# A mixture-of-experts, Mamba and soft-routing kernel: the routing chain's place among the first products on VectorE and TensorE, and five TensorE products on zeros ahead of the first inputs

## The reference, cut to what matters

```python
shared_out = jnp.einsum('nh,dh->nd', jax.nn.silu(x_flat @ sw1.T) * (x_flat @ sw3.T), sw2)
t_bias = t_emb @ router_t_w.T
s = jax.nn.sigmoid((x_flat @ router_w.T + t_bias_flat).astype(jnp.float32))
sel_scores = s + router_bias
_, topk_idx = jax.lax.top_k(sel_scores, TOP_K)
s_sel = jnp.take_along_axis(s, topk_idx, axis=1)
denom = jnp.sum(s_sel, axis=1, keepdims=True)
gates = jnp.where(denom > EPS, s_sel / (denom + EPS), 1.0 / TOP_K)
combine = jnp.sum(gates[:, :, None] * jax.nn.one_hot(topk_idx, N_EXPERTS), axis=1)
H = jax.nn.gelu(jnp.einsum('nd,ehd->enh', x_flat, rw1), approximate=False)
O = jnp.einsum('enh,edh->end', H, rw2)
routed_out = jnp.einsum('end,ne->nd', O, combine)
out = (shared_out + routed_out) / (N_SHARED + TOP_K)
```

## Time and profile before

| what | before |
|---|---|
| median of 3 runs | 1472.04 us (1471.96, 1472.04, 1476.65) |
| the profiled execution | 1476.72 us |
| its span | 1474.9 us |
| PE busy | 1184.5 us, 80% |
| DVE busy | 1149.8 us, 78% |
| ACT busy | 771.7 us, 52% |
| POOL busy | 884.9 us, 60% |
| first stage | about 0 to 187 us |
| the Mamba stage, by the busy shares | about 187 to 1160 us |
| what the change touches | 3.6 to 50 us |

### The profile page before, as it was taken

How to read it: one execution, slowest core, us unless ns; L and a number is a source line. 1 busy time by engine, 2 the same in 40 slices (tenths; PEclk the granted TensorE clock), 3 DMA queues, 4 the chain that set the end, 5 groups by cost and what they waited for, 6 DMA issues and landing times. The chain is left out here.

```text
span 1474.9 us, 14736 instructions
## 1 busy us (share of the span) xinstructions
PE 1184.5 (80%) x4924; PEld 659.2 (45%) x4924; DVE 1149.8 (78%) x1051; ACT 771.7 (52%) x1029; POOL 884.9 (60%) x394
## 2 busy tenths in 40 slices
PE   5999986797639897549986475484598999999998
PEld 3788832232103232113332121131146788787887
DVE  4344459999999999999999999999878654545445
ACT  4444466667645776555775555465256533343330
POOL 4530027999999999999999999999910000000000
PEclk9999998899959898769898678687799999999999
DMA  5344235442463234255123437313015030303012
GB/s 200 107 155 136 95 97 201 157 159 75 162 235 134 99 139 155 101 205 199 72 86 146 154 118 291 142 58 114 13 47 200 24 120 1 143 0 128 0 38 76
DMA packets 46016, 176.34 MB, mean 120 GB/s; under 512 B 5873, under 2 KB 10481, under 8 KB 33538
## 3 DMA queue, kind: packets, MB, share of 16 engines
q1 hardware_dynamic: 45954, 175.57, 32.8%
HBM read 142.78 MB, written 32.77 MB: 119 GB/s over the span
## 5 line engine op out<-in xcount | busy, mean ns | idle before, releaser
L1268 POOL TENSOR_TENSOR scan_dbu<-scan_rep,scan_bc 128x1024 f32<-128x1024 f32 x254 | 592.7, 2361 | 39.6 <-ACT scan_rep L1166 28.7
L1355 DVE TENSOR_TENSOR_SCAN scan_hs<-scan_hs,scan_dbu 128x1024 f32<-128x1024 f32 x191 | 436.7, 2286 | 11.6 <-ACT scan_hs L1193 10.1
L1193 ACT ACTIVATE scan_hs<-scan_rep,scan_neg_a 128x1024 f32<-128x1024 f32 x252 | 280.8, 1118 | 306.1 <-DVE scan_hc L1369 278.7
L1077 PE MATMUL scan_ysum<-scan_hc,scan_sel 128*32 128x512 f32 x1008 | 171.3, 812 | 206.5 <-DVE scan_hc L1369 190.3
L1369 DVE TENSOR_TENSOR scan_hc<-scan_hs,scan_bc 128x1024 f32<-128x1024 f32 x191 | 233.7, 1223 | 6.1
L1077 PEld LDWEIGHTS scan_ysum<-scan_hc,scan_sel 128*32 128x32 f32 x1008 | 35.5, 131 | 320.1 <-issue 269.5
L1274 POOL TENSOR_TENSOR scan_hc<-scan_hc,scan_bc 128x1024 f32<-128x1024 f32 x65 | 153.1, 2356 | 7.6 <-DVE scan_hc L1355 7.4
L1355 DVE TENSOR_TENSOR_SCAN scan_hc<-scan_hs,scan_dbu 128x1024 f32<-128x1024 f32 x65 | 148.1, 2279 | 0.8 <-POOL scan_dbu L1268 0.7
L938 PE MATMUL scan_banks<-late_xin,scan_inwf 128*128 128x512 f32 x256 | 115.2, 604 | 0.0
L32 PE MATMUL ffn_sl<-ffn_tanh_s,xm_s 128*128 128x512 f32 x384 | 107.3, 415 | 2.3 <-DVE ffn_tanh_s L2153 2.3
L1955 PE MATMUL ffn_oy<-ffn_y,ffn_et 128*128 128x256 f32 x448 | 102.0, 379 | 0.8 <-DVE ffn_y L2173 0.8
(11 more groups left out here) (274 smaller groups left out, 1820.4 us busy)
## 6 DMA issues: line engine op xcount, KB each, us to landing
scan_rep<-dd_rows SPq DMA_DIRECT2D x60, 1024.0 KB, 5.7
scan_bc<-bc_rows SPq DMA_DIRECT2D x32, 512.0 KB, 6.0
ffn_wt<-in_ew SPq DMA_DIRECT2D x16, 1024.0 KB, 7.8
dd_rows<-scan_dd SPq DMA_DIRECT2D x15, 1024.0 KB, 3.8
scan_bc<-gate_rows SPq DMA_DIRECT2D x24, 256.0 KB, 4.8
scan_inwf<-fold SPq DMA_DIRECT2D x12, 512.0 KB, 3.8
cond<-scan_bc SPq DMA_DIRECT2D x16, 256.0 KB, 3.1
y_all<-scan_yo SPq DMA_DIRECT2D x6, 512.0 KB, 3.1
```

Of the source, the lines that this page charges most:

```text
L1077: mm = nc.tensor.matmul(ysum[i * D32:(i + 1) * D32, h, :], sel[:], hc[:, (s0 + i) % HCR, h * CT:(h + 1) * CT], start=False, stop=last, til ...
L1193: nc.scalar.activation(hs[:, s % HSR, :], rep[:, e % REPS, 0, :], ACT.Exp, scale=scale).then_inc(da_done, 1)
L1268: nc.gpsimd.tensor_tensor(dbu[:, s % DBR, :], rep[:, e % REPS, 1, :], bc[:, j, 0, :], ALU.mult).then_inc(dbu_done, 1)
L1355: nc.vector.tensor_tensor_scan(states, hs[:, s % HSR, :], dbu[:, s % DBR, :], 0.0, ALU.mult, ALU.add).then_inc(scan_done, 1)
```

## The change

Three things are edited, all in the first stage.

- TensorE runs five products of 128x128 by 128x512 in plain float32 on the zeroed tile comb_wide, after the small products for t_emb and ahead of `value(0)`. It waits for padded first. They write to the bank by_expert, which `logits()` overwrites later; nothing reads what they give.
- VectorE does `low_hidden(0)` ahead of the 14 comparisons, `low_hidden(1)` and `product(2)` right after the rank, `low_hidden(2)` and `product(3)` where `low_hidden(1)` and `product(2)` were, and `low_hidden(3)` before the wait for the turned gates.
- TensorE runs `turn_gates()` two steps later: after `project(2)`, `value(5)` and `project(3)`; `factor(4)` follows `value(6)`.

```diff
@@ TensorE, the start
             mm.then_inc(t_done, 1)
+            pe.wait_ge(padded, 1)
+            for _ in range(IDLE_PRODUCTS):
+                zeros = comb_wide[:].rearrange("p t e -> p (t e)")
+                nc.tensor.matmul(by_expert, zeros[:, 0:P], zeros, start=True, stop=True)
+
@@ TensorE, the order of the first units
             value(4)
-            turn_gates()
             project(2)
             value(5)
+            project(3)
+            turn_gates()
+            value(6)
             factor(4)
-            project(3)
-            value(6)
             factor(5)
@@ VectorE, the routing chain
             link(nc.vector.tensor_tensor(score[:], prob[:], bias[:].unsqueeze(1).to_broadcast([P, NT, EXPERTS]), ALU.add))
-
+            low_hidden(0)
             for e in range(EXPERTS):
...
-            low_hidden(0)
             product(1)
             dve.wait_ge(padded, 1 + EXPERTS)
             dve.wait_ge(chain, links[0])
             link(nc.vector.tensor_reduce(rank[:], beats, AX_X, ALU.add))
+            low_hidden(1)
+            product(2)
             link(nc.vector.tensor_scalar(mask[:], rank[:], float(TOP_K), None, ALU.is_lt))
...
-            low_hidden(1)
-            product(2)
+            low_hidden(2)
+            product(3)
             link(nc.vector.tensor_scalar(den[:], den[:], 1e-9, None, ALU.add))
...
             nc.vector.tensor_tensor(comb, comb, mask[:], ALU.add).then_inc(comb_ready, 1)
-            low_hidden(2)
-            product(3)
+            low_hidden(3)
             dve.wait_ge(gates_turned, 1)
...
-            low_hidden(3)
```

More of the change, by code:

```diff
@@ L59, in moe_phase @@
         HB = 4
+        IDLE_PRODUCTS = 5
         flat = ahead.bc[:].rearrange("p j i t -> p (j i t)")
```

## The result

The kernels were timed side by side, 20 executions each: before 1476.96 us in the median (1471.96 to 1480.91), changed 1472.76 us (1468.33 to 1474.52). The profiled execution spans 4.5 us less, with 22 instructions more. The forecast of 1470.4 us was a gain of 1.6 us on a baseline 4.9 us lower than the one measured beside the change; in us gained it was too small by 2.6.

What follows compares the result with a forecast made beforehand. The first stage was taken as bound by TensorE once routing is over, with waits and half clock ahead of that. Start 1.6 plus middle 0.1 gave 1.7, stated as 1.6: 1472.04 - 1.6 = 1470.4 us, range 1465.8 to 1475.6.

Steps and rivals of the forecast that it cites:

- The start: Ahead of the logits: products on zeros raise TensorE's clock, so value(0) and factor(0) run faster and logits start 1.6 us earlier.
- C: Rival, first stage: the clock raised by the products falls again just ahead of the logits; slower, 1475.6 us; chance 0.14.
- D: Rival, at value(0): the products do nothing, the clock is half at 12.06 and rises where it did; 1472 us; chance 0.08.
- The meeting at 26.17: Last comparison and GpSimd's first rw1 split fall due together; forecast has the comparison first, otherwise the rank ends 2.3 us later.
- The last split: GpSimd's second half of rw2 begins at 33.84 instead of 41.75, stands on L489 or L490, and holds VectorE until 36.3.
- B: Rival, routing: L489 and L490 slip through before the last split, which must come 0.3 us later; 1465.8 us; chance 0.08.
- The wait at `project(2)`: TensorE waits from 32.0 to 37.4, 5.3 us, for low_hidden(2) and falls to 1.2 GHz.
- The sum: Whole kernel: 1.6 from the start plus 0.1 from the middle, 1.7, stated as 1.6 us less.
- The middle: From the logits to project(4): the reordering gives 0.1 us, with 0.8 either way for the clock.
- A: Rival, routing: GpSimd's split comes first at 26.17, the comparison waits, project(1) waits 2.0 us; 1468.6 us; chance 0.28.

Runs made afterwards that it cites:

- the products alone: The kernel before with only the five products on zeros added, both engines' orders as before; 1474.99 us, ratio 0.9997 to before.
- The experiment with 0.2 us more: The changed kernel with one more small VectorE step, its result overwritten, ahead of the 14 comparisons; 1474.44 us, a single execution.
- The run with the split earlier: The changed kernel with ScalarE's high part for the second half of rw2 ahead of hidden(4); 1475.6 us, ratio 0.9998 to before.
- the better order: The changed kernel with low_hidden(2) and product(3) ahead of the mask, rw2's last high half behind hidden(5), turn ahead of project(3); 1469.96 us, ratio 0.9955 to before.
- the run with the later split: The changed kernel with ScalarE's high part for the second half of rw2 behind high_hidden(3); 1472.39 us, ratio 0.9988 to before.
- the order alone: The changed kernel without the five products on zeros; 1475.25 us, ratio 1.0004 to before.
- the run with the turn as before: The changed kernel with TensorE's order as in the kernel before, turn_gates directly behind value(4); 1476.03 us, ratio 1.0008 to before.

## Why the prediction was right and wrong

**The start: right.** 1.6 us forecast, 1.43 measured at the logits. The products end at 10.89, inside the 8.3 to 12.7; `value(0)` takes 1.63, the logits start at 15.79 for 15.6: `factor(0)`, from 14.20, needed 1.59 us for a forecast 1.4. Rivals C and D fall for five products, as the clock held over the waits of 1.16 and 0.52; with two products C's mechanism is there. The size hangs on when the clock rises without such work. The three runs without five products have their logits at 17.22, 17.44 and 16.32, the seven with them at 15.75 to 15.96, so the products give 0.4 to 1.7 us. The gain reached the end of the stage, by the products alone 2.1 us at the next stage's first product.

**The meeting at 26.17: right as forecast, though the prediction said that its rows can't part the two cases.** The comparison came first, the rank is at 25.52 where the 26.95 - 1.43 of the prediction put it, and `project(1)` at 27.80 has no wait. The experiment with 0.2 us more shows how thin that was: it gives the other case. It also bears on what the Trainium skill says ("SBUF — State Buffer", section "Who interferes with whom"), that whoever issues first keeps the shared ports for its whole length; the traces agree, 2.00 us for the comparisons on one side of the meeting, 4.25 on the other. The prediction's own rule, that a routing step stands when all its operands lie in SBUF, is too wide: the rank L489 doesn't (1.21 us beside a split, 1.22 before).

**The last split: this step failed.** The prediction put it at 33.84 in before's count, 32.2 in the changed kernel's, and concluded of L489 and L490 that "both can't be through before it". It began at 32.98. Its start came out of `value(4)` by a chain: `hidden(4)`, ScalarE's half, then the split; and I had `value(4)` follow `project(1)` at once. It does not: `value(4)` needs rw1, whose splits end at 24.75 + 4.87 = 29.62, and it starts at 29.67 though `project(1)` was done by 29.3. The code says so (a wait on `split_done` in `value`), and the earlier trace rows held the time, 30.93 in before's count. I had used that row for VectorE and not for TensorE. The wait is marked as 0.35 us and moves `value(4)` by 0.51: it starts at 29.67 and not at 27.80 + 1.36 = 29.16, where 1.36 is the time of six matmuls from start to start. Of the 0.74 us by which the split came later than forecast it is the largest part; the rest is `project(1)` at 27.80 for 27.7 and `hidden(4)`, 1.69 us behind `value(4)`'s start for a forecast 1.56. Without those 0.51 the split would have begun at 32.47, level with L496. B's condition was that the split comes late ("0.3 us later than I have it"), and B's mechanism is what came, half: L489 and L490 (now L496 and L497) slipped through, 0.17 us each, but the step behind the next low part, L500, then stood for it, 1.31 us. So `project(4)` is at 45.19, between B's 43.4 and the forecast's 47.9.

**The wait at `project(2)`: wrong by the same step.** 5.3 us forecast at half clock, 2.30 measured at full clock. The run with the split earlier has the forecast's mechanism and its half clock, and there the wait is 3.98: `project(2)` starts at 35.52 for a forecast 37.4 - 1.6 = 35.8, but `value(4)` ends at 31.54, not at 32.0 - 1.6 = 30.4. It is the overlooked wait again. The prediction had said what would refute it: "I'm wrong if the wait at `project(2)` is under 3 us with a short last comparison". That is what came, so its account of the middle is wrong, though the time lies in the range.

**The sum.** The middle was put at 0.1 and gave 2.94. With the start 4.4 us instead of 1.7. The range held the time (1472.76 in 1465.8 to 1475.6), but that the forecast of 1470.4 came within 2.4 of it is partly luck: it was 1.6 below a median of three executions at 1472.04, and the median of 20 beside the change is 1476.96. The prediction had named the 4.7 us between that median and the profiled execution and left it open. Against the profiled execution, 1476.72, the forecast was 1475.1; the changed kernel's profiled execution took 1472.15.

**A misreading without effect.** The prediction says that none of TensorE's first three waits is for data that is not there. The first of them is: `value(0)` waits for the low part of sw1, which VectorE makes from weights that have only just arrived.

**The chances.** B had 0.08, "since the split hangs on TensorE's stream, which has no slack there". Its condition was a start 0.3 us later, at the end of a chain of five steps that I had built from durations; that is less than such a chain can be trusted for, as the meeting of comparison and split was treated (0.42 and 0.28). B should have had about what A had.

## What to carry to other kernels

Before saying which of two steps on two engines comes first, write down every wait of each and look up its time in the trace, also where it ends long before: a step that moves 5 us ahead meets waits that cost nothing where it was. If an engine's short steps stand still beside another engine's long operation, let the steps that don't stand (here those that read PSUM, and the rank) run then; with the last split and the turn moved too this gave 3.6 us in the better order, and an order that only brings data early gave 0.1 while the consumer waited for something else. Work on zeros ahead of the first inputs pays where it lasts until shortly before they arrive: five products left 1.16 us idle and kept the clock, two left 4.34 and lost it again.

## What the runs showed of the hardware

**A waiting step gets in between two splits that follow each other at once.** In the changed kernel the mask L492 is issued at 27.96, while the split pair of 24.75 runs, and ends at 29.70, just behind it, though GpSimd's next split starts at 29.58. The next step, L493, then stands for that whole split (2.37 us). It is so in the five other runs whose mask is issued during the pair (1.74 to 1.76 us each). Where the gap is 1.02 us, as ahead of the last split, L494, L496 and L497 get in.

**How long a wait keeps the clock is not settled by its length alone.** 2.30 us at `project(2)` kept it in the changed kernel (1.65 us behind it), and 2.29 in the run with the later split and in that with two products; 2.29 us at the same place lost it a little later in the order alone (1.91, then 2.76 for the next). With the comparisons pushed even 1.99 us lost it (1.85, then 2.76), while 2.23 us ahead of `value(0)` kept it in the run with the turn as before (1.61). 2.39 us lost it in the kernel before; 3.66, 3.98 and 5.56 lost it each time. I don't know what decides between 1.99 and 2.39.

**The executions of one kernel differ by more than this change is worth**, and TensorE's clock goes with it. The changed kernel's 20 lie at 1468.3 where the mean granted clock of the execution is 0.904, at 1470.5 to 1473.4 for 0.900 and 0.901, at 1473.3 to 1474.5 for 0.892 to 0.895 (the four at 0.897 and 0.898 lie at 1472.5 to 1473.6). In the ten profiled executions what lies behind VectorE's last scan instruction agrees to 0.3 us (363.8 to 364.1), while from the next stage's first product to there it takes 923.6 to 927.2: the scatter arises in the scan stage. Hence the table's last column, and hence the timed medians that can't be told from before although `project(4)` was 1.4 to 3.4 us earlier (products alone, order alone, last split earlier, turn as before). For the order alone, the later split and the turn as before the intervals (at most 1.3, 4.0 and 1.0 us less) leave out even the gain of their own profiled spans (2.0, 5.3 and 2.8 us). A part is that each span is one draw from this scatter; the rest I can't explain, and it stays open. Whether it matters at which moment the scan begins was not tried. So the timings show that the change and the better order are faster than before; what the parts give, and why, rests on the starts in the profiles, one execution each.
